# Two layer norms on VectorE: variances ahead of the centering, and the norm's offset ahead of x_lo

## The reference

```python
out = where(c == 0, nr(x), where(c == 1, tsr(x), where(c == 2, sr(x), 0)))
# nr, tsr: gelu(x w1 + b1) w2 + b2        sr: three layers, 256 -> 512 -> 256 -> 256
y = x + out
y = (y - mean(y)) * rsqrt(var(y) + 1e-5) * gamma + beta
h = gelu(y down_W^T + down_b)
h = h Wsel[d]^T + bsel[d] + domain_emb[d]
z = y + h up_W^T + up_b
out = (z - mean(z)) * rsqrt(var(z) + 1e-5) * ln_gamma + ln_beta
```

## Time and profile before

| | |
|---|---|
| median of 3 runs | 270.54 us (270.42 to 270.87) |
| profiled execution | 270.59 us, span 268.8 us |
| TensorE busy | 251.5 us, 94% |
| VectorE busy | 208.9 us, 78% |
| ScalarE busy | 191.2 us, 71% |
| GpSimd busy | 177.4 us, 66% |
| granted TensorE clock | 0.991 of full speed |

### The profile page before, as it was taken

How to read it: one execution, slowest core, us unless ns; L and a number is a source line. 1 busy time by engine, 2 the same in 40 slices (tenths; PEclk the granted TensorE clock), 3 DMA queues, 4 the chain that set the end, 5 groups by cost and what they waited for, 6 DMA issues and landing times.

```text
span 268.8 us, 8023 instructions
## 1 busy us (share of the span) xinstructions
PE 251.5 (94%) x2114; PEld 220.7 (82%) x2115; DVE 208.9 (78%) x717; ACT 191.2 (71%) x450; POOL 177.4 (66%) x188
## 2 busy tenths in 40 slices
PE   7998999999999998899999999999999999999970
PEld 6698898999999987788888888888788898888640
DVE  6769643474774674899999998998898989898894
ACT  3578479578678676687777777778687877778650
POOL 3134374463776775877777778777878787878551
PEclk9999999999999999999999999999999999999996
DMA  6372011011112112133332323323232322322315
GB/s 200 86 261 62 12 41 43 4 42 41 43 41 78 39 39 78 41 92 82 88 85 81 93 82 87 88 78 87 78 89 80 95 78 78 98 79 69 76 44 121
DMA packets 41639, 20.71 MB, mean 77 GB/s; under 512 B 37430, under 2 KB 39180, under 8 KB 41613
## 3 DMA queue, kind: packets, MB, share of 16 engines
q1 hardware_dynamic: 37625, 12.10, 18.6%
q0 software_dynamic: 2592, 7.08, 7.5%
q10 hardware_dynamic: 1396, 1.19, 1.7%
HBM read 11.69 MB, written 8.65 MB: 76 GB/s over the span
## 4 chain that ended last, share of the span: by engine, by line
PE 43%; DVE 17%; issue 15%; POOL 10%; ACT 7%; DVEq 4%; DMA 1%; ACTq 0%; POOLq 0%
PE ps_h L1089 14%; POOL h_lo L482 6%; PE ps_t L1179 5%; PE ps_z L1162 5%; POOL rs L489 4%; PE ps_z L1157 4%; DVE st L691 3%; PE ps_u L1209 3%; DVE n L727 3%; DVEq L338 2%; PE ps_t L1260 2%; PE ps_z L1124 2%; ACT yt L937 2%; DVE o L767 2%; PE ps_t L1263 2%
## 5 line engine op out<-in xcount | busy, mean ns | idle before, releaser
L482 POOL TENSOR_TENSOR h_lo<-h,h_hi 128x256 fp32r<-128x256 f32 (+1 forms) x75 | 73.3, 978 | 37.6 <-ACT h L903 35.1
L489 POOL TENSOR_TENSOR rs<-ve,minus_half 128x4 f32<-128x4 f32 (+1 forms) x38 | 38.2, 1005 | 31.6 <-DVE ve L703 31.4
L910 ACT ACTIVATE zn<-ps_z,nm,rs 128x256 f32<-128x256 f32 x66 | 33.7, 560 | 32.9 <-DVE nm L707 27.7
L691 DVE BATCH_NORM_STATS2 st<-ps_z 128x6 f32<-128x256 f32 x66 | 24.8, 415 | 32.7 <-PE ps_z L1162 32.7
L903 ACT ACTIVATE h_hi<-ps_h,per_feature_sb 128x256 fp32r<-128x256 f32 x84 | 38.6, 492 | 10.2 <-PE ps_h L1089 6.0
L937 ACT ACTIVATE yt<-ps_t,per_feature_sb 128x256 f32<-128x256 f32 x66 | 34.0, 573 | 10.1 <-PE ps_t L1179 9.6
L903 ACT ACTIVATE h<-ps_h,per_feature_sb 128x256 f32<-128x256 f32 x84 | 38.7, 498 | 0.0
L508 POOL DMA_INDIRECT out<-o,out_rows_now x27 | 34.2, 1267 | 4.7 <-issue 4.7
L1209 PE MATMUL ps_u<-tables,stack 65*64 x132 | 35.5, 392 | 0.3 <-ACT stack L921 0.3
L1209 PE MATMUL ps_u<-second_table,stack 65*64 65x256 f32 x132 | 35.6, 392 | 0.0
L1157 PE MATMUL ps_z<-last_hi,h_hi 128*128 (+1 forms) x132 | 35.4, 304 | 0.0
(11 more groups left out here) (150 smaller groups left out, 657.6 us busy)
## 6 DMA issues: line engine op xcount, KB each, us to landing
x<-in_x_feat SPq DMA_DIRECT2D x130, 64.0 KB
out<-o SPq DMA_DIRECT2D x18, 64.0 KB, 2.2
out<-o,out_rows_now POOLq DMA_INDIRECT x54
last_sb<-in_last_w SPq DMA_DIRECT2D x1, 768.0 KB, 5.1
w_sr_sb<-in_w_sr SPq DMA_DIRECT2D x1, 512.0 KB, 3.3
w_sr_sb<-in_w_sr ACTq DMA_DIRECT2D x1, 512.0 KB, 4.5
w_two_sb<-in_w_two SPq DMA_DIRECT2D x1, 512.0 KB, 5.7
out<-o ACTq DMA_DIRECT2D x6, 64.0 KB, 2.3
```

What stands on the lines that cost most here:

```text
L482: pool.tensor_tensor(dst, full, high.bitcast(F32), ALU.subtract).then_inc(ready, 1)
L489: pool.tensor_tensor(RS[p][:, norms, :], VE[p][:, norms, :], half_of_two[:, norms, :], ALU.pow).then_inc(rstd, 1)
L910: ins = act.activation(ZN[:, t, :], ZP[p][:, t, :], ACT.Identity, bias=NM[p][:, t:t + 1], scale=RS[p][:, 0, t:t + 1])
```

## The change

In VectorE's step of all slots but the last two, the centering n moves from ahead of mv and ve to behind them, and nm moves from behind the second norm's mv to between st of ps_u and x_lo. Nothing else is changed, and the other engines' instructions are the same in the same order.

```diff
                 for slot in on_slot(g, 0, where):
                     first_stats(slot, p)
-                for slot in on_slot(g, 3, where):
-                    center(slot, q, p)
                 for slot in on_slot(g, 0, where):
                     first_moments(slot, p)
                 variances(p, BOTH)
+                for slot in on_slot(g, 3, where):
+                    center(slot, q, p)
                 for slot in on_slot(g, 2, where):
                     second_stats(slot, p)
+                for slot in on_slot(g, 0, where):
+                    minus_mean(slot, p, where)
                 for slot in on_slot(g, -2, where):
                     input_low(slot, p)
                 for slot in on_slot(g, 2, where):
                     second_moments(slot, p, q)
                     if where == LAST2:
                         dve.wait_ge(stat[1], 2 * TT * slot + 2 * TT)
                         variances(q, SECOND)
-                for slot in on_slot(g, 0, where):
-                    minus_mean(slot, p, where)
                 for slot in on_slot(g, 3, where):
                     finish(slot, i - 2 if p == 0 else i - 1, q, where)
```

## The result

The changed kernel takes 280.28 us in the median of 4 runs (278.73 to 282.44), against 270.54 before (270.42 to 270.87): slower, by a ratio of 1.0373 (95% interval 1.0333 to 1.0412). 264.8 was forecast, with a range of 263.0 to 268.0. The profiled execution has a span of 278.1 us, 9.3 more than before.

The account below looks back on a forecast made before the run. TensorE was taken to bound the three-layer stretch, and TensorE with stalls on h_lo the two-layer one. Against the profiled 270.59 us, -5.5 (pace), -0.4 (first slots) and +0.2 (x wait) gave 264.9, median 264.8; range 263.0 to 268.0.

Parts of the forecast that it names:

- x_lo is made a whole step ahead: nothing: Three-layer stretch: x_lo comes later by most of an h_lo each step, but its lead covers that; cost put at nothing.
- The rival on the slower side: Two-layer steps: nm and x_lo reach the port before h_lo, TensorE waits, pace 6.45, 6.6 us slower, 277.1 us; chance 7%.
- TensorE's own step: Two-layer stretch: the pace TensorE keeps when nothing stalls it, 5.85 us; with it the forecast pace was 5.90.
- steps without a stall: Two-layer stretch before the change: seven intervals between ps_z groups, 5.80 to 5.88 us, read as starting after a stall and meeting none.
- The power leaves the ring: Two-layer step: with ve 0.53 us earlier, h_lo waits for ScalarE's h, no longer for rs (the power), and ends 0.32 earlier.
- The ring of 5.78 us: Two-layer stretch: VectorE's cycle from one h_lo to the next, through x_lo, mv, st, ve, rs and h_lo, summed to 5.78 us.
- What limits next. Two things: Two-layer stretch after the change: VectorE's cycle of 5.78 us or TensorE's step of 5.85, the larger setting the pace; 5.90 taken.
- VectorE keeps the pace: Rival, two-layer stretch: VectorE's cycle is really 6.0 us because of nm behind h_lo and the statistics' wait; 267.1 us, chance 12%.
- st of ps_u without its wait for u: Sign of being wrong, VectorE's step: this wait, 0.31 us in the step shown, vanishing would mean that VectorE sets the pace.
- the passage: Between the three-layer and two-layer stretches: TensorE's wait for x, 0.76 us, grows by 0.2; over 1 us would show it wrong.
- The rule of the port: VectorE instructions with two SBUF inputs and GpSimd ones reading SBUF exclude each other; nm, then x_lo, wait until h_lo ends, 151.96.
- The first slots: At 36 us, without centering: nm ahead of x_lo takes 0.35 off rs in two steps; 0.4 us gained, ends 0 and 0.7.

Follow-up runs that it names:

- the run by kind: Changed kernel, but with the order of before while the slot whose x_lo is made is a three-layer one: 267.91 us, ratio 0.9877 against before.

## Why the prediction was wrong

**The step that failed** is "x_lo is made a whole step ahead: nothing", in the part on the three-layer stretch. I had seen there that x_lo and the bias would come later "by most of an h_lo in each step", and that TensorE is full; both held. The lead was read from the numbering of the slots, and by the rows that I did not look up there was none: TensorE began 0.07 us behind x_lo's end, as close as it comes when it waits for it. VectorE's step g starts when TensorE's step g ends, and what it makes is used a half layer later. Two sizes follow from that, 1.2 us of delay times the steps with centering and 1.9 to 2.35 in the first two. Their sum was 9.0 us of waits, and with the clock and the restarts 11.5. With the order of before there, or with x_lo first, the waits are gone, and with them the loss but for about 1 us, in single steps that have other causes.

**The rival on the slower side was the wrong one.** It gave 277.1 and a mechanism that did not occur: no step of the changed kernel has x_lo ahead of h_lo. That the sign came from a stretch that I had put at nothing means that the 6% for slower did not stand for what happened.

**The centering's move** by itself did what the prediction worked out. rs comes 1.45 instead of 1.98 us behind st (0.53, to the digit), TensorE's waits for h_lo are gone in the two-layer stretch, and the pace of 5.79 is better than the 5.85 that I took for TensorE's own step. That term was mis-sized: the seven "steps without a stall" were not free of the one before them. In them ps_h starts 0.56 to 0.58 us behind the ps_z group, in the steps of 5.72 to 5.76 without a stall 0.46.

**The move of nm** was put at nothing; in the two-layer stretch it costs 0.23 us a step (6.02 against 5.79), and in the three-layer stretch and the head it adds to the loss. nm did behave as said: 0.48 long, ended by h_lo, with x_lo back to 0.68 behind it, and ScalarE's zn earlier. "The power leaves the ring" did not hold in the changed kernel: h_lo started at the end of rs in every two-layer step and never waited for ScalarE's h. The ring of 5.78 us was short of a term: from ve to rs I had 0.25, and it measured 0.61 (148.75 to 149.36), since ve now met the first h_lo. With that and nm out of the ring (0.13), 5.78 + 0.36 - 0.13 = 6.01. And "What limits next. Two things" left out a third, GpSimd's own order: the stores grew from 1.28 and 0.96 to 1.36 and 1.54, and with that it was full as well. The rival "VectorE keeps the pace" had the size, 6.0, but not this cause, since it put the excess down to nm and the statistics. Which of the two full engines alone would set 6.02 the runs do not separate. One sign of being wrong that the prediction named is there, st of ps_u without its wait for u (10.7 us in 22 waits before, none printed between 121 and 254 us after), and so are the new waits for x_lo and a wait for x at the passage of 1.08 us.

**The rule of the port** (the Trainium skill, SBUF — State Buffer, section "Who interferes with whom") held where I used it: x_lo at 58.27, with only the centering moved, lasts 1.53 beside h_lo, and the pair of n keeps its 0.85 to 0.88 in the changed kernel, beside h_lo or not. The same section of the Trainium skill bears on what I missed. It says that tensor_scalar and copies, when their operands meet some conditions, can take both ports in a fast mode and then exclude a GpSimd instruction, also one that prepares a DMA. The traces are in line with it: ve, a tensor_scalar of four columns, went from 0.17 to 0.53 beside h_lo, and the second store from 0.96 to 1.54 beside the bias and the copies. That these ran in that mode no run here shows. I had put only nm and x_lo on the list of those that can collide.

**The first slots** went as said for rs (1.03 at 28.33 instead of 1.39), and it was worthless: TensorE waited 2.35 us for x_lo there.

## What to carry to other kernels

A lead that follows from slot numbers is not a lead in time: before an instruction is moved back, look in the trace at when its result is used, in every stage, and above all in the one in which the consumer is full and shows no wait. A consumer that starts right behind the result, at the distance that it has elsewhere after a wait, has no lead. Count as a limit the order of every engine in the loop, also of one that has a fifth of its time free now. A stage that can't be made faster can still be made slower. And when two engines share a port, list every instruction on either side that can use it, the one-column ones too; moving one of them moves which pairs meet.

## What the runs showed of the hardware that was not expected

An instruction of four columns (ve) can be held for 0.36 us by another engine's subtraction, and an indirect store by GpSimd lasts 0.96, 1.14, 1.18 or 1.54 us depending on what VectorE runs beside it, with the same rows stored in all.

TensorE's granted clock went from 1.00 to 0.79 of full speed between 41 and 46 us and 0.87 from 46 to 51, so to its lower level for part of that time, in the step with the wait of 1.88 us behind an earlier one of 2.35. It fell in the same two windows of the traces of nm's move alone, of the copies ahead of the bias, of the copies of one column and of the copies ahead of the outputs, all with waits of 2.35 to 2.38 and 1.87 to 1.92. With waits of 2.21 and 1.73, in the profiled execution of the kernel without ve, the clock stayed at 1.00 and the step took 11.1 us instead of 12.8. But one execution of the changed kernel, not traced, had a mean clock of 0.993 over its span, more than the 0.991 of the kernel before, so the order of the calls alone does not make it fall. In the run by kind it fell to 0.71 between 26 and 31 us, with TensorE busy all of the 10 us before but for one wait of 0.74, which the kernel before had at the same place at a clock of 1.00. What decides it stays open.
